# Three float32r products, or plain fp32 in four column tiles, for fc1, q and k of a macaron block

## The reference, cut to what matters

```python
x = x + 0.5 * ffn(layernorm(x)); x = x + attn(layernorm(x)); x = x + 0.5 * ffn(layernorm(x))
# ffn(x): h = LN(x) * ln_gamma + ln_beta
#         z = silu(h @ w1 + fc1_bias) @ w2 + fc2_bias       w1 128x512, w2 512x128, both dequantised
#         returns x + 0.5 * z
# attn(x): qkv = x @ w_qkv; 16 heads of 8; w = relu(q k^T / sqrt(8)); w / (sum(w) + 1e-6) @ v
#          y = x + out @ w_out + b_out; LN(y) * gamma + beta
```

## Time and profile before

| | |
|---|---|
| median of 3 runs | 370.05 us (369.62 to 370.37) |
| profiled execution, first to last instruction | 369.5 us |
| PE busy | 360.0 us (97%), 4518 matmul records |
| DVE busy | 283.8 us (77%) |
| ACT busy | 231.4 us (63%) |
| POOL busy | 219.8 us (59%) |
| PE's granted clock | nine tenths of full speed or more in all 40 slices |

### The profile page before, as it was taken

How to read it: one execution, slowest core, us unless ns; L and a number is a source line. 1 busy time by engine, 2 the same in 40 slices (tenths; PEclk the granted TensorE clock), 3 DMA queues, 4 the chain that set the end, 5 groups by cost and what they waited for, 6 DMA issues and landing times.

```text
span 369.5 us, 11752 instructions
## 1 busy us (share of the span) xinstructions
PE 360.0 (97%) x4518; PEld 185.2 (50%) x4518; DVE 283.8 (77%) x689; ACT 231.4 (63%) x425; POOL 219.8 (59%) x447
## 2 busy tenths in 40 slices
PE   8999998999999999999999999999999999999996
PEld 8854433453564445653564434644456535532476
DVE  5876677897778977699777977689776797578774
ACT  3377465667847586466865678475864668588523
POOL 7595065547973589437992479635894377315541
PEclk9999999999999999999999999999999999999999
DMA  7016005500351005500173003610063001710001
GB/s 211 4 31 173 3 0 128 131 3 2 88 143 60 3 0 136 147 8 1 31 173 87 4 0 67 165 59 2 4 156 104 4 0 32 191 38 2 2 2 61
DMA packets 14103, 22.66 MB, mean 61 GB/s; under 512 B 2528, under 2 KB 3808, under 8 KB 14048
## 3 DMA queue, kind: packets, MB, share of 16 engines
q1 hardware_dynamic: 11456, 17.83, 20.1%
q10 hardware_dynamic: 2592, 4.07, 3.4%
HBM read 3.54 MB, written 2.10 MB: 15 GB/s over the span
## 4 chain that ended last, share of the span: by engine, by line
PE 87%; DVE 4%; ACT 2%; DMA 2%; issue 2%; POOL 2%; SPq 0%; POOLq 0%; DVEq 0%; ACTq 0%
PE o_bank L682 30%; PE scores L659 16%; PE pre_bank L603 9%; PE post_bank L603 9%; PE pre_bank L608 5%; PE pre_bank L609 3%; DMA q_op<-q_parts 2%; PE pre_bank L631 2%; PE post_bank L608 2%; PE pre_bank L596 1%; PE post_bank L609 1%; PE post_bank L631 1%; PE o_bank L590 1%; PE post_bank L596 1%; PE scores L608 1%
## 5 line engine op out<-in xcount | busy, mean ns | idle before, releaser
L1280 DVE TENSOR_SCALAR probs<-scores 128x512 f32<-128x512 f32 x242 | 155.8, 683 | 48.3 <-PE scores L659 45.0
L981 ACT ACTIVATE probs<-scores 128x512 f32<-128x512 f32 x262 | 141.7, 596 | 65.9 <-PE scores L659 65.9
L682 PE MATMUL o_bank<-probs,v_op 128*32 128x512 f32 x1024 | 135.9, 602 | 0.2
L659 PE MATMUL scores<-q_op,k_op 32*128 32x512 f32 x504 | 76.0, 494 | 1.9 <-DMA q_op<-q_parts 0.8
L659 PEld LDWEIGHTS scores<-q_op,k_op 32*128 32x128 f32 x504 | 31.9, 181 | 81.5 <-issue 54.4
L870 ACT ACTIVATE pre_y<-pre_bank,b_sum,col_consts 128x512 f32<-128x512 f32 x28 | 21.9, 782 | 23.6 <-PE pre_bank L631 23.5
L682 PEld LDWEIGHTS o_bank<-probs,v_op 128*32 128x32 f32 x1024 | 21.9, 108 | 28.4 <-issue 24.6
L603 PE MATMUL pre_bank<-w,pre_y 128*32 128x128 f32 x960 | 30.8, 274 | 0.0
L603 PEld LDWEIGHTS pre_bank<-w,pre_y 128*32 128x32 f32 x960 | 25.7, 110 | 8.1 <-issue 7.7
L603 PE MATMUL post_bank<-w,post_y 128*32 128x128 f32 x960 | 29.3, 273 | 0.0
L603 PEld LDWEIGHTS post_bank<-w,post_y 128*32 128x32 f32 x960 | 25.9, 110 | 5.6 <-issue 5.4
(11 more groups left out here) (219 smaller groups left out, 555.3 us busy)
## 6 DMA issues: line engine op xcount, KB each, us to landing
k_op<-k_parts SPq DMA_DIRECT2D x62, 128.0 KB, 2.7
q_op<-q_parts SPq DMA_DIRECT2D x62, 128.0 KB, 2.7
out_dram<-o_rows ACTq DMA_DIRECT2D x7, 256.0 KB, 2.0
pre_x<-in_x_dram ACTq DMA_DIRECT2D x6, 256.0 KB, 2.8
w_int<-in_L_ffn_fc_q_dram SPq DMA_DIRECT2D x2, 256.0 KB, 3.9
rows<-in_lines_dram ACTq DMA_DIRECT2D x1, 256.0 KB, 6.0
s_rows<-in_L_ffn_fc_scales_dram SPq DMA_DIRECT2D x1, 256.0 KB, 6.6
wqk<-in_w_qk_dram SPq DMA_DIRECT2D x1, 256.0 KB, 6.7
```

The lines of the kernel that those rows point to most:

```text
L659: mm(score_bank(b, s, i, j), k_op[rows, g, P * kt:P * (kt + 1)], q_op[rows, g, :], start=True, stop=True).then_inc(scores_done[i], 1)
L682: last = mm(o_bank[pair][VW * j:VW * (j + 1), :], v_op[:, kt, heads_of(g).start + 2 * j, :], probs[:, s % 2, j, :], start=(odd == 0 and kt ...
L981: activation(probs[:, s % 2, 2 * i + j, :], score_bank(b, s, i, j), ACT.Relu).then_inc(probs_done[i][j], 1)
L1280: v.tensor_scalar(probs[:, s % 2, 2 * i + j, :], score_bank(b, s, i, j), 0.0, None, ALU.max).then_inc(probs_done[i][j], 1)
```

## The change

fc1, q and k become one plain fp32 product each, in four column tiles: the 128 columns of the stationary weights in four parts of 32, each with all tokens moving, out on 32 PSUM partitions. There is no split of weights or tokens any more: ACT's copy out of PSUM gives `t` (fp32), `w1_whole` is w1 times gamma in fp32, `wqk` is used as it was loaded. DVE's and POOL's subtractions, ACT's second copy of u, and the making of `w1_lo`, `wqk_hi` and `wqk_lo` are gone. `weights.b1` is made in column tiles too, and stands ahead of the first transposes. The order at the two ends follows; in the middle, the lists of PE and ACT are as before and entries go from DVE's and POOL's.

```diff
 PE_FIRST = [
-    "warm_up.11", "first.hT.0", "weights.b1", "first.hT.1", "first.fc1.0.0", "first.low.0.0", "first.fc1.1.0",
...
-    "first.low.3.1", "first.fc2.0.0", "first.fc2.0.1", "first.fc2.1.0", "first.fc2.2.0", "first.fc2.3.0",
-    "first.fc2.1.1", "first.fc2.2.1", "first.fc2.3.1", "warm_up.8", "first.uT.0", "first.k0.0", "first.uT.1",
-    "first.k0_low.0", "first.q0.0", "first.q0_low.0", "first.q0.1", "first.q0_low.1", "first.v.0", "first.k0.1",
-    "first.k0_low.1"
+    "warm_up.11", "weights.b1", "first.hT.0", "first.hT.1", "first.fc1.0.0", "first.fc1.1.0", "first.fc1.0.1",
+    "first.fc1.2.0", "first.fc1.1.1", "first.fc1.3.0", "first.fc1.2.1", "first.fc1.3.1", "first.fc2.0.0",
+    "first.fc2.0.1", "first.fc2.1.0", "first.fc2.2.0", "first.fc2.3.0", "first.fc2.1.1", "first.fc2.2.1",
+    "first.fc2.3.1", "warm_up.8", "first.uT.0", "first.k0.0", "first.q0.0", "first.uT.1", "first.q0.1", "first.v.0",
+    "first.k0.1"
 ]
 DVE_ORDER = [
...
-    ["post.hT@-1"],
+    [],
     [],
     ["oT.0", "den.0", "pre.k_lo@1"],
     ["pre.q_lo@1"],
     ["a.0"],
-    ["pre.hT@2"],
+    [],
 ]
 POOL_ORDER = [
...
-    ["pre.x_stats@2", "pre.uT@1"],
+    ["pre.x_stats@2"],
...
-            def two_products(into, w_hi, w_lo, t_hi):
-
-                mm(into, w_hi, t_hi, start=True, stop=False)
-                mm(into, w_lo, t_hi, start=False, stop=False)
+            def by_columns(into, w, tokens):
+
+                for j in range(HG):
+                    part = slice(VW * j, VW * (j + 1))
+                    last = mm(into[part, :], w[:, part], tokens, start=True, stop=True)
+                return last
...
-                    two_products(into, w1_hi[:, cols], w1_lo[:, cols], st.t_hi[:, :])
-                    mm(into, w1_hi[:, cols], st.t_lo[:, :], start=False, stop=True).then_inc(st.full, 1)
+                    by_columns(into, w1_whole[:, cols], st.t[:, :]).then_inc(st.full, 1)
...
-                        pe.wait_ge(u_hi_in, b + 1)
-                        two_products(pre.bank[:, :], wqk_hi[:, i, :], wqk_lo[:, i, :], pre.t_hi[:, :])
-                        pe.wait_ge(u_lo_in, b + 1)
-                        mm(pre.bank[:, :], wqk_hi[:, i, :], pre.t_lo[:, :], start=False, stop=True).then_inc(pre.full, 1)
+                        by_columns(pre.bank[:, :], wqk[:, i, :], t_u[:, :]).then_inc(pre.full, 1)
...
-                    last = mm(o_bank[0][:, f:f + 1], w1[:, P * f:P * (f + 1)], be_col, start=True, stop=True)
+                    last = by_columns(o_bank[0][:, f:f + 1], w1[:, P * f:P * (f + 1)], be_col)
...
                         act.wait_ge(q_made, 1)
-
-                    activation(st.t_hi[:, :], st.bank[:, :], ACT.Copy).then_inc(st.t_hi_in, 1)
+                        act.wait_ge(*emptied(pre, 1, "k"))
+
+                    activation(st.t[:, :], st.bank[:, :], ACT.Copy).then_inc(st.free, 1)
...
-                        activation(pre.t_hi[:, :], pre.bank[:, :], ACT.Copy).then_inc(u_hi_in, 1)
                         activation(t_u[:, :], pre.bank[:, :], ACT.Copy).then_inc(pre.free, 1)
...
-            def low_t(st, hi_in, count, done):
-                dve.wait_ge(hi_in, count)
-                v.tensor_tensor(st.t_lo[:, :], st.bank[:, :], st.t_hi[:, :].bitcast(F32), ALU.subtract
-                                ).then_inc(done, 1)
...
-                    elif what == "uT":
-                        pool.wait_ge(pre.free, len(PRE_FILLS) * b + pre.n("uT"))
-                        p.tensor_tensor(pre.t_lo[:, :], t_u[:, :], pre.t_hi[:, :].bitcast(F32), ALU.subtract
-                                        ).then_inc(u_lo_in, 1)
```

More of the change, by code:

```diff
@@ L112 @@
     "post.fc1.3@-2", "post.fc2.0@-2", "post.fc2.1@-2", "post.fc2.2@-2", "post.fc2.3@-2", "last.hT.0@-1",
[L113 to L117, removed]
+    "last.fc1.0.0@-1", "last.fc1.1.0@-1", "last.fc1.2.0@-1", "last.fc1.3.0@-1", "last.hT.1@-1", "last.fc1.0.1@-1",
+    "last.fc1.1.1@-1", "last.fc1.2.1@-1", "last.fc1.3.1@-1", "last.fc2.0.0@-1", "last.fc2.0.1@-1", "last.fc2.1.0@-1",
+    "last.fc2.2.0@-1", "last.fc2.1.1@-1", "last.fc2.3.0@-1", "last.fc2.2.1@-1", "last.fc2.3.1@-1"
 ])
 ACT_FIRST = [
-    "weights.w1_hi", "first.hT.0", "first.hT.1", "first.fc1.0.1", "first.fc1.1.1",
-    "first.fc1.2.1", "first.fc1.3.1", "first.uT.0", "first.t_u.0", "first.uT.1", "first.k0.0", "first.q0.0",
-    "first.t_u.1", "first.q0.1", "first.v.0", "first.k0.1"
+    "weights.w1", "first.hT.0", "first.hT.1", "first.fc1.0.1", "first.fc1.1.1", "first.fc1.2.1", "first.fc1.3.1",
+    "first.uT.0", "first.uT.1", "first.k0.0", "first.q0.0", "first.q0.1", "first.v.0", "first.k0.1"
 ]
@@ L182 @@
 DVE_FIRST = [
[L183 to L186, removed]
+    "weights.slots", "first.x_stats.0", "first.x_stats.1", "weights.w1", "first.x_apply.0", "first.x_apply.1",
+    "weights.b1", "weights.w2", "pre.x_stats@1", "first.xr.1", "first.x1.0", "first.x1_stats.0", "first.x1.1",
+    "first.x1_stats.1", "first.u_apply.0", "first.u_apply.1", "first.k0.0", "first.q0.0", "first.q0.1", "first.k0.1"
 ]
@@ L189 @@
     ["first.k_lo.1"],
-    ["pre.hT@1", "first.q_lo.1"],
+    ["first.q_lo.1"],
     [],
@@ L239 @@
     ["den.0"],
-    ["a.0", "post.hT@-1"],
+    ["a.0"],
 ]
@@ L244 @@
     "last.x2.0@-1", "last.x2_stats.0@-1", "last.y_apply.1@-1", "last.x2.1@-1", "last.x_apply.0@-1",
-    "last.x2_stats.1@-1", "last.hT.0@-1", "last.x_apply.1@-1", "last.hT.1@-1", "post.out@-2", "last.xr.0@-1",
+    "last.x2_stats.1@-1", "last.x_apply.1@-1", "post.out@-2", "last.xr.0@-1",
     "last.xr.1@-1", "last.out.0@-1", "last.out.1@-1"
@@ L451, in first_bank @@
             return scores[1][:, h, cols_of(h)] if i == 0 else (scores[0][:, 0, :], o_bank[0])[h][:, cols_of(h)]
-        def first_high(i):
-            return (post.t_hi, post.t_lo)[i]
+        first_high = [sb(f"first_{n}_high", [P, S], F32R) for n in "qk"]
         def copied(g, b):
@@ L750, in edge @@
                         pe.wait_ge(post.free, len(POST_FILLS) * (b - 1) + post.n(f"fc1.{f}"))
[L751 to L756, removed]
+                    by_columns(to, w1_whole[:, weights], st.t[:, cols]).then_inc(done, 1)
                 elif what.startswith("fc2"):
@@ L920, in edge @@
                     act.wait_ge(*filled(st, h, "hT"))
-                    activation(st.t_hi[:, cols], turn_bank(st, h)[:, cols], ACT.Copy).then_inc(st.t_hi_in if h else st.t_hi_a, 1)
+                    activation(st.t[:, cols], turn_bank(st, h)[:, cols], ACT.Copy
+                               ).then_inc(last_free if h == 1 and st is post else done, 1)
                 elif what.startswith("fc1"):
@@ L930, in edge @@
                     act.wait_ge(*filled(pre, h, "uT"))
-                    activation(pre.t_hi[:, cols], into[:, cols], ACT.Copy).then_inc(u_hi_in if h else u_hi_a, 1)
-                elif what == "t_u":
-                    act.wait_ge(*of_half(u_lo_a, u_lo_in, h, b))
                     activation(t_u[:, cols], into[:, cols], ACT.Copy).then_inc(done, 1)
@@ L1086, in task @@
                         row_stats(norm_x, b, pre.x(b))
-                    elif what == "hT":
-                        low_t(pre, pre.t_hi_in, b + 1, pre.free)
                     elif what == "x1":
@@ L1127, in task @@
                         row_stats(norm_x2, b, post.x(b))
-                    elif what == "hT":
-                        low_t(post, post.t_hi_in, b + 1, post.free)
                     elif what == "out":
```

67 lines of the change are left out of this document (18 added, 49 removed).

## The result

The changed kernel takes 373.61 us (373.15 to 373.97, 4 runs) against 370.21 of before in the same comparison: a ratio of 1.0089, 95% interval 1.0074 to 1.0105, slower by 0.9%. The forecast was 373.7.

A forecast was written before the change was run, and what follows sets the result against it. PE bounds the middle, a chain through all engines the two ends. Middle +3.65, batch 0 -1.15, head +0.55 and end +0.65 make +3.7 us on the profiled 369.5; with 0.55 above span, 373.7, range 371.9 to 375.6.

The forecast's parts named there:

- The group's price: One product in four column tiles on PE: 0.88 us ahead of column tiles, 0.99 ahead of anything else.
- The rival of a cheaper group by its shared tokens: Four tiles moving the same 512 token columns cost 0.80, not 0.88, over 66 groups: 368.4 us; 6%.
- that of a dearer one: Four new stationary parts or the one shared source make a group 0.94 on average: 377.7 us; 9%.
- A middle batch: PE alone in batches 2 to 6: +0.59 us each; batch 1 +0.70; sum +3.65.
- Steps 12 and 13: Middle batch, values and two products: 2.59 us becomes 2.75, +0.16 each.
- Step 11: Middle batch, transposes of u and one product: 1.28 us becomes 1.52, +0.24.
- Step 15: Middle batch, one product between scores and transposes: 0.81 us becomes 0.99, +0.18.
- Step 1: Middle batch, three fc2 parts and one product: 2.76 + 0.89 becomes 2.65 + 0.88 us, -0.12.
- the rival that forecast a faster kernel: Less DVE and ACT work ends scores' waits in light steps, up to 7.5 us less: 366.2; 6%.
- Batch 0: PE's waits of 0.49 and 0.45 us for low parts end, with 0.2 of restarts: -1.15.
- The head: Kernel start: beta's product 1.1 us, fc1 at about 8.5 (+0.2), half groups +0.26, late transposes +0.1: +0.55.
- The end: Output projection 0.3 us late, then second half's transposes 0.35 to 0.4 later behind fc1: +0.65.

The follow-up runs named there:

- the second comparison: The changed kernel measured and profiled again against the kernel before, also run again: 374.33 us, ratio 1.0110.
- the swap in step 11: Changed kernel with fc1.0 of `post` put ahead of the transposes of u on PE, against the kernel before: 373.33 us, ratio 1.0077.

## Why the prediction was right

The time came out within 0.1 of the forecast (0.6 above it in the second comparison), and the mechanism is the one forecast, but that it is as close as 0.1 is luck. By the second pair of profiles the head is 0.37 and the end 0.18 above the forecast, and batch 0 is 0.58 below it.

- *PE is the bound in the middle.* Right: all other engines lost work and the middle batches got longer.
- *The group's price.* Right within 0.02: 0.88 forecast, 0.86 to 0.88 measured ahead of column tiles; 0.99 forecast, 0.97 behind column tiles and 0.99 to 1.00 behind scores or transposes. The rival of a cheaper group by its shared tokens was real only by those 0.02, that of a dearer one falls.
- *A middle batch.* +0.59 forecast, +0.42 to +0.68 measured (2.77 over five batches). Steps 12 and 13: 0.16 forecast, 0.10 to 0.14. Step 11: 0.24 forecast, 0.28 to 0.32. Step 15: 0.18 forecast, 0.24 to 0.26, where no wait for a q falls in one of the two profiles. The transposes in these two steps were mis-sized: 0.53 was taken from the earlier trace rows, where they stand behind a set; behind column tiles they take 0.59. Step 1: -0.12 forecast, -0.17 or -0.18; steps 2 and 3: nearly 0 forecast, about -0.04 each. Too dear and too cheap by step nearly cancel. Batch 6 is not like the others, which the prediction overlooked: no transposes stand in its step 15, which changes by -0.04 instead of +0.18, and its step 13 gets 0.29 to 0.34 longer, as q's group stands 1.07 behind the values instead of 0.88: it waits for DVE to take k out of the bank that it writes (L1054, done at 311.75, q's group at 311.80).
- *Relief of the other engines is worth nothing in the middle.* Right, and with it the rival that forecast a faster kernel falls: the long scores of step 8 have the same length in the changed kernel within 0.02, in every batch from 1 to 6.
- *Switches.* The Trainium skill's rule (TensorEngine Tiling, Key Properties) is that a change of tiling mode drains the engine. The runs agree that such a change costs time: 0.14 in step 11 for the same work, and with fc1 of `post` alone 0.3 in steps 12 and 13, where a flat price gave 0.06; whether that time is a drain no trace shows. The prediction's estimate of 0.166 per switch had given +0.9 per batch; the rows' own prices gave 0.59, and the measured 0.55 is by the rows.
- *Batch 0.* -1.15 forecast, -1.87 and -1.73 measured. The two waits went as forecast (-0.5 in step 1, -0.75 in step 12, +0.13 in step 13). The term that was mis-sized is what the prediction put at nothing: the first scores of batch 1 stand 0.6 to 0.8 earlier still, in step 15, as q's second issue takes 2.98 and 3.15 to land instead of 3.78. With the same lists up to there, the swap in step 11 had only 0.25 of it, so its size is that of an execution and not of the change alone.
- *The head.* +0.55 forecast, +0.45 and +0.92 measured, on two pairs of executions whose early pace differed. The parts were not what I had said: beta's product is 0.54, not 1.1 (below the 0.88 that was given as the least), so that fc1 starts at 8.12, not 8.5; the late transposes of u cost 0.43, not 0.1, since ACT's copy and q0's second half wait for them in turn.
- *The end.* +0.65 forecast; 0.65 and 0.66 from the last scores to the last group of PE, in the two places named: 0.42 up to the output projection and 0.38 between the transposes of the two halves, of which 0.13 comes back behind them. Up to the projection the three groups account for 0.14 only; 0.28 lies between the bias product and the first group, which stand 0.63 apart where it was 0.35. Another 0.26 to 0.28 is lost in step 12 of batch 7, where nothing was changed on PE. In it PE's values wait 0.18 for DVE's relu (at 343.06). The cause stays open. Behind PE's last group the changed kernel's profiles are 0.25 and 0.10 shorter, which the prediction did not have either.
- *The offset.* The prediction set the runs 0.55 above the span. It is 1.8 to 1.9; the profile at hand was long by 1.2. The sum was of differences, so the forecast time stood, but a reader who compares the two spans, 369.5 and 371.8, would find only 2.3 of 3.4.

## What to carry to other kernels

Where PE is saturated, cost a matmul from start to start together with its neighbours' tiling, and change a product's form only where that removes a switch or ends a wait: here one fp32 product in four column tiles was as cheap as three float32r products between other column tiles, or up to 0.18 a step cheaper, and 0.1 to 0.3 dearer next to row tiles, transposes or another product of the old form. Outside batch 0, do not read the split of the operands as the cost to be saved; the subtractions ran on engines that had time. Profile the base twice before a difference of under 1% is worked out from spans.

## What I had not expected of the hardware

- The 16 plain fp32 matmuls (32 records) of beta's product, with one moving column in column tiles, took 0.54 us (0.37 in the second profile), 12 to 17 ns a record; the 0.0275 us a record that I had held for a floor is one of 128 moving columns.
- The moment at which PE's pace doubles in the head moved between executions of one kernel, from 7.8 to 6.2 us, and took 0.76 us of the first scores' start with it, while the granted clock reads 1.000 for both.
- Transposes of four 128x128 tiles take 0.41, 0.53 or 0.59 us from start to start, depending on their neighbours.
- The second issue of a transfer of q (two issues of 128 KB) took 2.62 to 3.91 us to land, at one place of the program in eight kernels, 2.98 or more in the seven traces where a 16 KB packet of an instruction queue ran and ended in that time, and at most 2.65 in the other three.
